# A DLRM tower with thirteen tables held in SBUF, three one-hot slots and GpSimd gathers in rows of 7, 6, 7 and 6

## What is computed

```python
# 26 tables of 128 columns; 13 of them have 1000 rows, the others 1250, 12500 or 125000
e = jnp.stack([tbl_0[ids[:, 0]], tbl_1[ids[:, 1]], ..., tbl_25[ids[:, 25]]], axis=1)
combined = jnp.concatenate([dense[:, None, :], e], axis=1)            # 27 features of 128
interactions = jnp.einsum('bfd,bgd->bfg', combined, combined)
z = interactions[:, iu, ju]                                           # 351 pairs
h = jnp.concatenate([z, dense], axis=1)                               # 479
h = jnp.maximum(h @ W_top1 + b_top1, 0.0)                             # 512
h = jnp.maximum(h @ W_top2 + b_top2, 0.0)                             # 256
y = h @ W_top3                                                        # 1
```

## Time and profile before

| | |
|---|---|
| median of three runs | 468.56 us (459.24 to 474.06) |
| profiled execution | 465.19 us, span 463.4 us |
| TensorE busy | 393.1 us, 85% of the span |
| VectorE, ScalarE, GpSimd busy | 281.4, 158.7, 221.6 us |
| mean granted TensorE clock | 0.918 of full |

### The profile page before, as it was taken

One profiled execution on the slowest core, in us unless ns is written; L12 is line 12 of the kernel. 1 busy time (PEld: TensorE's weight loads), 2 busy tenths in 40 slices (PEclk: granted clock), 3 DMA queues, 4 the chain that ended last, 5 costly groups with the idle time before them and its releaser, 6 DMA issues.

```text
span 463.4 us, 14600 instructions
## 1 busy us (share of the span) xinstructions
PE 393.1 (85%) x6452; PEld 360.9 (78%) x6452; DVE 281.4 (61%) x195; ACT 158.7 (34%) x270; POOL 221.6 (48%) x228
## 2 busy tenths in 40 slices
PE   1999487988879998888989699798995799888996
PEld 1889476977669897788889588696895698777885
DVE  4899995927439385773795166481885438583230
ACT  2275610434213342225522253133431144122532
POOL 5757545642356526563157623664266622666000
PEclk9999968898888999799998979799997789979999
DMA  7997132211222113211231113221132102311300
GB/s 180 267 251 235 28 92 62 71 43 28 86 55 68 40 34 107 68 45 28 79 85 45 45 31 91 57 64 34 34 110 66 45 17 62 84 45 45 106 21 11
DMA packets 23135, 34.35 MB, mean 74 GB/s; under 512 B 6127, under 2 KB 14959, under 8 KB 23115
## 3 DMA queue, kind: packets, MB, share of 16 engines
q1 hardware_dynamic: 15762, 19.30, 14.7%
q0 software_dynamic: 7168, 14.69, 12.3%
q10 hardware_dynamic: 186, 0.09, 0.1%
HBM read 30.97 MB, written 0.01 MB: 67 GB/s over the span
## 4 chain that ended last, share of the span: by engine, by line
PE 68%; issue 12%; DMA 7%; SPq 5%; another core or an unknown queue 3%; ACT 2%; POOL 1%; DVE 1%; ACTq 0%; POOLq 0%; DVEq 0%
PE psum L536 39%; PE psum L562 9%; PE psum L551 5%; DMA lows<-table 4%; PE psum L652 4%; SPq L197 3%; PE psum L575 3%; PE psum L576 3%; PE psum L577 3%; PE psum L524 2%; SPq L230 1%; DMA pairs<-gram 1%; DMA rows<-table,idx 1%; ACT feats L401 1%
## 5 line engine op out<-in xcount | busy, mean ns | idle before, releaser
L289 POOL DMA_INDIRECT rows<-table,idx x224 | 221.4, 988 | 207.4 <-issue 76.4
L317 DVE TENSOR_TENSOR onehot<-ids_b,psum 125x2048 fp32r<-125x2048 int16 x96 | 216.0, 2284 | 67.7 <-remote 40.7
L401 ACT ACTIVATE feats<-psum 128x512 f32<-128x512 f32 (+2 forms) x120 | 81.5, 711 | 206.1 <-remote 138.7
L536 PE MATMUL psum<-onehot,hot_hi 125*128 125x256 f32 x728 | 122.5, 306 | 22.3 <-issue 18.2
L536 PEld LDWEIGHTS psum<-onehot,hot_hi 125*128 125x128 f32 x728 | 105.1, 207 | 31.4 <-issue 30.7
L536 PE MATMUL psum<-onehot,hot_lo 125*128 125x256 f32 x728 | 115.7, 301 | 6.1 <-issue 5.9
L536 PEld LDWEIGHTS psum<-onehot,hot_lo 125*128 125x128 f32 x728 | 104.4, 208 | 9.2 <-issue 9.0
L297 DVE COPY gram<-psum 26x416 f32<-26x416 f32 x64 | 37.4, 584 | 94.4 <-PE psum L562 76.2
L562 PE MATMUL psum<-feats 128*26 128x26 f32 x4096 | 48.5, 196 | 17.5 <-issue 14.0
L562 PEld LDWEIGHTS psum<-feats 128*26 128x26 f32 x4096 | 43.9, 107 | 23.9 <-issue 19.0
L401 ACT ACTIVATE gram<-psum 26x416 f32<-26x416 f32 (+1 forms) x72 | 35.6, 495 | 36.4 <-DMA pairs<-gram 27.5
(11 more groups left out here) (36 smaller groups left out, 170.5 us busy)
## 6 DMA issues: line engine op xcount, KB each, us to landing
lows<-table SPq DMA_DIRECT2D x12, 448.0 KB
ids_b<-hot_ids SPq DMA_DIRECT2D x8, 512.0 KB
rows<-table,idx POOLq DMA_INDIRECT x224, 2.5
ids_b<-hot_ids SPq DMA_DIRECT2D x8, 256.0 KB
lows<-w SPq DMA_DIRECT2D x2, 1024.0 KB, 5.3
rows<-dense SPq DMA_DIRECT2D x16, 64.0 KB
lows<-table SPq DMA_DIRECT2D x12, 52.0 KB
pairs<-gram SPq DMA_DIRECT2D x16, 39.0 KB
```

The costliest lines, as they stand in the source:

```text
L289: pool.indirect_dma_start(out=rows[:, f, :], out_offset=None, in_=tables[f - 1], in_offset=bass.IndirectOffsetOnAxis(ap=idx[:, 2 * s + t, ...
L317: nc.vector.tensor_tensor(onehot[f % SLOTS][0:HP_ROWS, :, :], ids_b[0:HP_ROWS, f:f + 1, :].to_broadcast([HP_ROWS, HC, SB]), psum[0:HP_ROWS ...
L401: return nc.scalar.activation(o, x, ACT.Copy)
L536: mm = nc.tensor.matmul(psum[:, bank, m * SB:(m + 1) * SB], part[0:HP_ROWS, f, c, :], onehot[f % SLOTS][0:HP_ROWS, c, :], start=(part is h ...
```

## The change

- `NUM_HOT` is 13, so the last table with 1000 rows is held too, and 13 features are gathered per tile instead of 14. TensorE gets 16 matmuls more per turn and two transpositions less, VectorE one compare more.
- `SLOTS` is 3 instead of 4. The ids of a turn arrive in two loads, of 3 and 10 tables (before: 4 and 8).
- `GROUPS` are features 0 to 3, 4 to 6, 7 to 10 and 11 to 13. Feature 0 is the dense one, which SP loads, so a tile's gathers are 3, 3, 4 and 3.
- The hot units are six pairs and one single; before they were five pairs and two singles. `WHOLE` has six tables.
- GpSimd's waits are new. Before group 1 of tile 0 it waits for the last gram of the turn before. Before group 3 of tile 0 it waits until group 2 has landed, before group 1 of tile 1 until group 0 has landed, each with all its gathers, and before group 3 of tile 1 it waits for tile 0's gram (in turn 0 too). Between these waits stand 7, 6, 7 and 6 gathers.

```diff
 from contextlib import ExitStack
 
 
-NUM_HOT = 12
+NUM_HOT = 13
 
 
 def dlrm_tower(nc, ids, dense, tables, ident, hot_ids, hot_tables, hot_rows, w1, b1, w2, b2, w3, out):
...
     HALF_K = 16
     SB = 2 * P
     HP_ROWS, HC = hot_rows.shape
-    SLOTS = 4
+    SLOTS = 3
     AHEAD = 4
     N1, N2 = w1.shape[1], w2.shape[1]
     C1, C2 = N1 // P, N2 // P
...
     ZP = max(FILL)
     MOVED = 16 * len(PIECES)
     RELUS = C1 + C2
-    GROUPS = [list(range(g, min(g + 4, NR))) for g in range(0, NR, 4)]
+    ENDS = (0, 4, 7, 11, NR)
+    GROUPS = [list(range(a, b)) for a, b in zip(ENDS, ENDS[1:])]
     NG = len(GROUPS)
     IDS_A = SLOTS
-
-    HOT = [[f, f + 1] for f in range(0, NH - 2, 2)] + [[NH - 2], [NH - 1]]
-
-    WHOLE = [0, 2, 4, 6, 8]
+    HOT = [list(range(f, min(f + 2, NH))) for f in range(0, NH, 2)]
+
+    WHOLE = [0, 2, 4, 6, 8, 10]
     SPLIT_ORDER = [f for f in range(NH) if f not in WHOLE] + WHOLE
     assert NG == 4 and len(HOT) == 7 and C1 == 4 and C2 == 2
 
...
             elif s > 0:
                 wait_rows(eng, s - 1, 1, g)
 
-        def wait_gathered(eng, s, t, g):
-
-            eng.wait_ge(gathered[t][g], 16 * (sum(f > 0 for f in GROUPS[g]) - 1) * (s + 1))
-
         def copy_gram(eng, copy, h, s, t, first):
             dst = gram[0:NJ, :].rearrange("i (j q h k) -> i j q h k", j=NJ, q=4, h=2)
 
...
         def _(pool):
             def wait_landed(s, t, g):
 
-                if g > 0:
-                    wait_gathered(pool, s, t, g - 1)
-                elif t == 0:
-                    wait_gathered(pool, s - 1, 1, NG - 1)
+                pool.wait_ge(gathered[t][g], 16 * sum(f > 0 for f in GROUPS[g]) * (s + 1))
+
+            def wait_gram(s, t):
+
+                pool.wait_ge(gram_done[1], 2 * s + t + 1)
 
             pool.wait_ge(idx_in, 16)
             for s in range(TURNS):
                 for t in range(2):
                     for g, features in enumerate(GROUPS):
                         wait_rows_free(pool, s, t, g)
-                        if s > 0:
-                            wait_landed(s, t, g)
-                        if s > 0 and t == 0 and g == 1:
-
-                            pool.wait_ge(gram_done[1], 2 * s)
+                        if s > 0 and (t, g) == (0, 1):
+                            wait_gram(s - 1, 1)
+                        elif s > 0 and (t, g) == (0, 3):
+                            wait_landed(s, 0, 2)
+                        elif s > 0 and (t, g) == (1, 1):
+                            wait_landed(s, 1, 0)
+                        elif (t, g) == (1, 3):
+                            wait_gram(s, 0)
                         for f in features:
                             if f > 0:
                                 pool.indirect_dma_start(
                                     out=rows[:, f, :], out_offset=None, in_=tables[f - 1],
                                     in_offset=bass.IndirectOffsetOnAxis(ap=idx[:, 2 * s + t, f - 1:f], axis=0),
-                                ).then_inc((gathered_last if f == features[-1] else gathered)[t][g], 16)
+                                ).then_inc(gathered[t][g], 16)
 
         @block.vector
         def _(dve):
...
                     copy_dense(s)
                 else:
                     rest_of_dense(s)
-                if not last:
-                    compare(s + 1, 3, False)
                 copy_gram(dve, copy, 1, s, 1, first)
 
             nc.vector.memset(pairs[:, :, :], 0.0).then_inc(zeroed, 1)
...
                 if g == 0 and not first:
 
                     act.wait_ge(dense_split, s)
-                copy(feats[:, t, :, 4 * g:4 * g + w],
+                copy(feats[:, t, :, GROUPS[g][0]:GROUPS[g][0] + w],
                      psum[:, bank, 0:w * P].rearrange("d (f n) -> d n f", f=w)).then_inc(feats_out, 1)
 
             def round_dense(s):
...
                 n, bank = place("rows", t, g)
                 if g == 0:
                     pe.wait_ge(dense_in[t], 16 * (s + 1))
-                wait_gathered(pe, s, t, g)
-                pe.wait_ge(gathered_last[t][g], 16 * (s + 1))
+                pe.wait_ge(gathered[t][g], 16 * sum(f > 0 for f in GROUPS[g]) * (s + 1))
                 wait_bank(s, n)
                 for m, f in enumerate(GROUPS[g]):
                     mm = nc.tensor.transpose(psum[:, bank, m * P:(m + 1) * P], rows[:, f, :], ident_sb[:, :])
```

7 lines of the change are left out of this document (3 added, 4 removed).

## The result

The changed kernel takes 492.78 us (median of four runs, 485.33 to 493.26), the one before in the same comparison 466.24 (459.24 to 474.06). The ratio is 1.0565, 95% interval [1.0478, 1.0653]: slower, where 451 was forecast. The profiled execution took 493.26 with a span of 491.4, 28.0 over that of before (463.4). Turn 1 starts 12.1 later (at 75.57, before at 63.44), the seven turns from it on take 16.2 more (57.05 us each instead of 54.74), and what follows them 0.3 less.

What follows compares the result with a forecast made beforehand. The first half was taken as bound by the round of compare, hot matmuls, late update, next compare. Profiled 465.2, -25.5 for seven turns, +7.5 for turn 0 give 447.2; with 3.4 to the median, 451 us, range 432 to 486.

Steps and rivals of the forecast that it cites:

- A full stop of GpSimd clears what has piled up; a stop of one microsecond does not.: First half: drawn from turn 4's 2.30 us pause against turn 3's 1.13; full stops were to bring 34.1 us to 32.0.
- seen 1.2 to 2.6 later by turns 4 and 3; I take 6.5: First row of seven: table 1, ended 4.0 us into the turn, is seen at 6.5; TensorE waits 0.5 for table 4's compare.
- seen at 27.5: Second row of seven: table 9's update, needed by table 12's compare, is seen at 27.5 us; first half ends at 32.0.
- the wait for late updates in the rows of seven: First half: compares wait for updates 1.2 us late or until the row lands; the half takes 32.0 us, from 34.1.
- late end of 30.5: Second row of seven: table 9's update seen only with the landing, at 30.5 us; first half would be 34.7.
- "Issue" gaps "nearly gone": Sign in the profile after: TensorE's idle issue in hot tables nearly vanishes and its clock comes nearer to 1.
- Second half 19.1: Second half: 17.3 us running free, plus 1.6 waiting for the last group and 0.2 for the copy; between 18.5 and 20.5.
- the row of seven has landed before layer 1a starts: Second half: gathers no longer run into layer 1 and the gram; the half before lost 3.3 us, much of it so.
- Turn 0 +7.5: Turn 0: 3.2 us for table work and transpositions plus 4.3 waiting behind tile 0's gram; 4.8 to 9.5.
- 4.3 over what TensorE has to do: Turn 0: rows arrive 8.6 us behind tile 0's gram, with a stretched 3.62 us gather, so TensorE waits 4.3.
- Three slots are too few: Rival: each compare depends on a table younger, 2 us less slack; first half 37.5, turn 56.6, time 489; chance 0.18.
- It is not the gathers: Rival: TensorE falters because of its own instruction stream, so losses stay; +24.5 + 7.5, time 500; chance 0.04.

Runs made afterwards that it cites:

- e7: Changed kernel with a full stop of GpSimd before every group but a tile's first, gram waits kept: 453.27 us, 0.982 of the kernel before.
- e13: e12 without the stop before group 2 of tile 0, so one row of seven returns: 456.45 us, 0.988 of the kernel before.
- e9: Kernel before with its stops made complete, each until the whole group before has landed: 482.99 us, 1.053 of the kernel before.
- e8: e7 with the wait for tile 0's gram replaced by one for the group before: 468.44 us, 1.019 of the kernel before.
- a0: Changed kernel unaltered, run again beside the kernel before: 490.22 us, ratio 1.057.
- e12: e7 with the wait for tile 0's gram only from turn 1 on: 444.67 us, 0.967 of the kernel before.
- e10: Kernel before with three slots instead of four, on a chip with late updates: 463.22 us, 1.011 of the kernel before.
- e11: Changed kernel without the gathers of turns 1 to 7, on a chip with late updates: 410.64 us, one run.
- e1: Kernel before given only GpSimd's new waits, on the 400 us chip: 411.47 us, 1.030 of the kernel before.
- e3: Changed kernel with the old waits between groups, on the 400 us chip: 412.34 us, 1.031 of the kernel before.
- e6: Changed kernel with the wait for tile 0's gram replaced by one for the group before: 467.31 us, 1.007 of the kernel before.
- e2: Kernel before with three slots instead of four, on the 400 us chip: 401.75 us, 1.006 of the kernel before.

## Why the prediction was wrong, step by step

- *"A full stop of GpSimd clears what has piled up; a stop of one microsecond does not."* Right where updates are late: all kernels with full stops and no row of seven in the first half have 28.5 to 31.3 us there.
- *Table 1's update "seen 1.2 to 2.6 later by turns 4 and 3; I take 6.5", and table 9's "seen at 27.5".* **This is the step that failed: the wait for late updates in the rows of seven.** The 1.2 to 2.6 come from rows of before that had a stop of 2.30 or 1.13 us after the fourth gather, and were carried into rows that have none. Table 1 was seen at 10.8, 6.75 late, with the landing. And the compare for table 11, which needs table 8, had no term at all. It is the one that ends the half: table 8 was seen at 30.7, 4.25 late, and behind it stand two compares, where the sum had one. In turn 2 table 1 was only 2.7 late, and the half still took 37.2 (TensorE had stood 4.54 us before table 6 there, for a copy that was let go only 1.5 us behind the row of six, and table 11's compare started at 30.5). The prediction knew the bound: its late end of 30.5, applied to table 8, gives 34.7 + 2.2 = 36.9; measured are 37.7. This account of table 11 is read from the traces; that shorter rows remove the loss is what e7 and e13 show.
- *"Issue" gaps "nearly gone".* Wrong, and the sum had no term for them. They came in all seven first rows, 7.1 to 7.9 us behind the first gather, where the earlier trace rows had shown them 8 us after a start, and a row of seven plus its landing is 10 us. They stretched four tables of turn 3 by 3.6 us, and the granted clock was 0.62 from 204 to 213 us; both lie in front of the last late update and so add nothing to its sum. The faltering and the late updates may be one thing; no run tells them apart.
- Together: 37.7 instead of 32.0, seven times 5.7 = 40 of the 46 us between the -18 forecast and the +28.1 measured.
- *Second half 19.1.* Right: 19.3 on average, and in turn 3 18.6 with 1.7 us of waiting for the last group. The mechanism, "the row of seven has landed before layer 1a starts", held too, and e9 and e8 show what it is worth.
- *Turn 0 +7.5.* Measured +12.1: 5.4 before tile 0's gram (3.1 had been taken) and 6.7 behind it. The wait for the rows, 3.55 beside the 4.3 taken, is right by luck. "4.3 over what TensorE has to do" leaves TensorE 4.3 of the 8.6 us to work, but turn 0 has no layer there: its transpositions took 2.5. And the stretched gather, 3.67 us, was the fourth, behind the rows that were waited for. In a0 it was the third, 4.56 us, and the wait 8.15. The second gram took 10.6 instead of 6.0 (6.7 in a0): it falters beside the last gathers of the row of six behind tile 0's gram, and 3.66 us of it are idle "issue" from 71.5 on, after the row has ended at 68.2; what holds it there is not shown. e12 puts the wait's price at 8 us of second half.
- *Rivals.* "Three slots are too few" had the numbers (first half 37.5, turn 56.6, 489), and the part of it on rows of seven is what came true: e7 keeps three slots and gains 37 us. What three slots add to such a row was not run (e10: 1.1% without one). Against "It is not the gathers" the prediction held that turn 4 of before does not falter; its trace has idle "issue" of 0.25, 0.22 and 0.32 us in hot tables at 253 to 257 us. e11 decides this rival without it.

The sum by measured terms: 465.2 + 12.1 + 7 x 2.31 = 493.5, against 493.26 profiled.

## What to carry to other kernels

A lateness read from a trace belongs to the pattern around it: before carrying it into a longer row, ask which pause let the update out, and bound it by the row's end. Stops of the gathering engine pay only if the gathers they push back meet nothing worse; write down where the last one lands (here: in a gram of 256 small matmuls). A wait that is put into every turn also stands in the first one; here leaving it out there took 8 us off that turn's second half.

## What was not expected of the hardware

- The same program takes 400 us on one chip and 457 to 466 on the others. On the first TensorE's updates are seen at once during gathers (six compares back to back), on the others up to 6.9 us late. The changed kernel without gathers takes 402 and 411. All the gains of stops are measured on the second kind; e12 was not run on the first, where e1 and e3 cost 3%.
- On the second kind TensorE stops issuing, mostly after some 60 matmuls behind a row's first gather (with the exceptions told above), and then gets one hot matmul, or five to six small ones, out per 0.73 us or more, until about a microsecond after the row. That it is a count of matmuls and not a time rests on comparison of traces; no run changed the count alone on such a chip. What in the chip holds TensorE up stays open, and so does why e6's first halves are 2 us shorter than the changed kernel's.
- The Trainium skill (TensorE: Matmul & The Clock Gate, "The cost: per-tile semaphore tail") puts a semaphore increment at some 26 ns. The first chip does not speak against it: in turn 3 of e2 the waiting compare starts 0.04 us after the modelled end of table 0. The 6.75 us of the others have no place in it.
- The Trainium skill (DMA: Bandwidth & Descriptors, "Rules for kernel authors") advises to issue a DMA early and wait late. Here issuing later, in short rows with full stops, took 37 us off the changed kernel's 490 (e7), and the same stops cost the kernel before 5% (e9).
